# Differential attention: the causal mask of the maxima pass, by VectorE in PSUM or by matmuls with the identity

## The reference, cut to what matters

```python
q = (x @ Wq).reshape(Bz, Tl, H, 2, D)      # H = 8, D = 32: 16 score maps a sequence of Tl = 512
k = (x @ Wk).reshape(Bz, Tl, H, 2, D)
v = (x @ Wv).reshape(Bz, Tl, H, 2 * D)
causal = jnp.tril(jnp.ones((Tl, Tl), dtype=bool))
def attend(qc, kc):
    s = jnp.einsum('bthd,bshd->bhts', qc, kc) * scale
    s = jnp.where(causal, s, -jnp.inf)
    a = jax.nn.softmax(s, axis=-1)
    return jnp.einsum('bhts,bshe->bthe', a, v)
o1, o2 = attend(q[..., 0, :], k[..., 0, :]), attend(q[..., 1, :], k[..., 1, :])
o = o1 - lam * o2                            # then a norm over 64 channels, g, and @ Wo
```

## Time and profile before

| What | Value |
|---|---|
| median of three runs | 2410.3 us (2406.4 to 2411.33) |
| the profiled execution: its time | 2407.47 us |
| its span, first to last instruction | 2405.7 us |
| PE busy | 2087.0 us (87%) |
| DVE busy | 1228.1 us (51%) |
| ACT busy | 749.2 us (31%) |
| mean granted TensorE clock | 0.903 |
| the four maxima stages begin at (first L2297) | 1148.3 us in the first chunk, 1910.67 us in the last |

### The profile page before, as it was taken

The page is one execution under the profiler, slowest core; times in us unless marked ns, Lnnn a source line. Parts: engine busy times, 40 slices in busy tenths (PEclk is TensorE's granted clock), DMA queues, the critical chain, the costliest instruction groups (busy, mean ns, idle before and its releaser), DMA issues. The chain is left out here.

```text
span 2405.7 us, 29600 instructions
## 1 busy us (share of the span) xinstructions
PE 2087.0 (87%) x12078; PEld 996.0 (41%) x12078; DVE 1228.1 (51%) x2281; ACT 749.2 (31%) x1163; POOL 221.2 (9%) x164
## 2 busy tenths in 40 slices
PE   4777486878877479999999999989998999999998
PEld 3444333333435234444444444434443444444443
DVE  5444445657554445555557445653566356623332
ACT  4444123333242122223234322442235123511211
POOL 3341021211110000000100010001000000000000
PEclk7777577988785589999999999999999999999999
DMA  6211402021112212222111111111111111222322
GB/s 247 88 53 18 164 10 48 22 37 28 31 49 58 93 55 94 97 97 75 41 43 62 36 62 54 53 45 53 53 54 53 53 39 34 78 88 98 114 92 74
DMA packets 90978, 158.75 MB, mean 66 GB/s; under 512 B 44182, under 2 KB 55772, under 8 KB 86108
## 3 DMA queue, kind: packets, MB, share of 16 engines
q1 hardware_dynamic: 90844, 156.86, 20.3%
HBM read 128.52 MB, written 18.87 MB: 61 GB/s over the span
## 5 line engine op out<-in xcount | busy, mean ns | idle before, releaser
L1130 PE MATMUL ps<-arena 128*128 128x512 f16 (+1 forms) x4512 | 1019.1, 381 | 19.8 <-DVE arena L1893 12.9
L1130 PEld LDWEIGHTS ps<-arena 128*128 128x128 f16 x4512 | 437.2, 99 | 541.4 <-issue 48.5
L1838 PE MATMUL ps<-arena 128*128 128x512 f16 x1536 | 348.9, 383 | 29.5 <-DVE arena L1884 16.3
L1838 PEld LDWEIGHTS ps<-arena 128*128 128x128 f16 x1536 | 147.4, 98 | 207.3 <-issue 29.2
L1860 ACT ACTIVATE arena<-ps,arena 128x512 f32<-128x512 f32 x128 | 87.6, 684 | 362.3 <-PE ps L1130 362.0
L1893 DVE SCALAR_TENSOR_TENSOR arena<-arena,ps 128x512 f32<-128x512 f32 x128 | 87.9, 686 | 210.1 <-ACT arena L1860 209.5
L2447 ACT ACTIVATE arena<-ps 128x1024 f32<-128x1024 f32 (+3 forms) x128 | 90.1, 704 | 253.7 <-PE ps L2356 253.7
L2552 DVE CAST arena<-arena 128x1024 f16<-128x1024 f32 (+3 forms) x128 | 66.6, 520 | 149.7 <-ACT arena L2447 147.7
L2518 DVE TENSOR_REDUCE arena<-ps 128x2 f32<-128x256 f32 (+3 forms) x128 | 99.6, 819 | 65.1 <-PE ps L2300 65.1
L1902 DVE SCALAR_TENSOR_TENSOR arena<-ps,arena 128x512 f32<-128x512 f32 x128 | 95.8, 748 | 39.3 <-PE ps L1130 39.1
L1921 DVE SCALAR_TENSOR_TENSOR arena<-ps,arena 128x512 f32<-128x512 f32 x64 | 44.0, 687 | 139.6 <-PE ps L1838 139.4
(11 more groups left out here) (267 smaller groups left out, 2466.5 us busy)
## 6 DMA issues: line engine op xcount, KB each, us to landing
arena<-wug_dram SPq DMA_DIRECT2D x128, 512.0 KB, 3.3
arena<-wd_hi_dram SPq DMA_DIRECT2D x16, 1024.0 KB, 5.0
arena<-wd_lo_dram SPq DMA_DIRECT2D x16, 1024.0 KB, 7.3
arena<-arena SPq DMA_DIRECT2D x144, 64.0 KB, 2.1
wug_dram<-arena SPq DMA_DIRECT2D x4, 2048.0 KB, 16.5
arena<-_attn_hidden_states_dram SPq DMA_DIRECT2D x4, 1024.0 KB, 11.8
arena<-in_L_ffn_W_up_dram SPq DMA_DIRECT2D x8, 512.0 KB, 4.4
arena<-in_L_ffn_W_down_dram SPq DMA_DIRECT2D x4, 1024.0 KB, 8.0
```

The lines of the kernel that those rows point to most:

```text
L1130: ins = pe.matmul(out, left[a](c), right[b](c), start=(at == 0), stop=(at == 3 * n - 1))
L1838: ins = pe.matmul(k.ps[:, bank, :], act[x][:, slot, cols], wd[y][:, f, :], start=(f == 0 and m == 0), stop=(f == 7 and m == 2))
```

## The change

On TensorE the four identity matmuls of each unit are gone, and c_score is raised by the score matmuls. On VectorE each of the two halves of a unit first adds the mask to the last 128 columns of its two banks, in place in PSUM, and then reduces the banks. A link stands between the two, since the reduction reads what the addition writes.

```diff
         for r in range(4):
             rows = slice(32 * r, 32 * r + 32)
-            pe.matmul(k.ps[:, max_bank(n, r), 0:w], k.qk_hi[rows, b, u * P:w], k.qk_hi[rows, 4 + b, 0:w],
-                      start=True, stop=False)
-        for r in range(4):
-            ins = pe.matmul(k.ps[:, max_bank(n, r), w - P:w], k.identb, k.causal_ts, start=False, stop=True)
+            ins = pe.matmul(k.ps[:, max_bank(n, r), 0:w], k.qk_hi[rows, b, u * P:w], k.qk_hi[rows, 4 + b, 0:w],
+                            start=True, stop=True)
             if r % 2:
                 ins.then_inc(s["c_score"], 1)
@@
             bank = max_bank(n, 2 * j)
             e.wait_ge(s["c_score"], 2 * UNITS * i + 2 * n + j + 1)
+            edge = k.ps[:, bank:bank + 2, u * P:(u + 1) * P]
+            V.link(e.tensor_tensor(edge, edge, bcast(k.causal_ts.unsqueeze(1), [P, 2, P]), ALU.add))
             e.tensor_reduce(k.mx[:, u, 4 * b + 2 * j:4 * b + 2 * j + 2], k.ps[:, bank:bank + 2, 0:(u + 1) * P], AXX,
                             ALU.max).then_inc(s["c_max"], 1)
```

## The result

The changed kernel takes 2434.23 us in the median of four runs (2431.96 to 2436.11), the kernel before 2410.17 (2406.4 to 2411.33, four runs). The ratio is 1.0105, with a 95% interval of 1.0089 to 1.0121: slower by 1.05%, and the medians lie 24.1 us apart. The forecast was 2441, the range 2423 to 2449.

A forecast was written before the change was run, and what follows sets the result against it. TensorE bounds the kernel, but waits for VectorE's reductions in loops of the maxima stages. Waits of 13.8 us plus clock loss of 17 make 31 us, added to 2410.3 for 2441 us; range 2423 to 2449.

The forecast's parts named there:

- The bound: Maxima stages: TensorE waits for VectorE's reductions in a loop, so VectorE's time counts there despite its 51% mean load.
- TensorE's saving: Identity matmuls removed from the maxima units: 0.23 us for each of 64 units, 14.7 us of TensorE time.
- The addition's price: VectorE's mask addition in PSUM: 0.418 us plus 0.035 for the link, x = 0.45 us each, two a unit.
- the case of a dear write: Rival: VectorE's write to PSUM makes x 0.55 to 0.7 us, giving 2446 to 2458 us; chance 0.10.
- The steps: Times between maxima units: unit 1 to 2 +0.74, 2 to 4 +0.62, 4 to 5 −0.23; a four-unit period +1.13 us.
- the sum: Maxima stage, clock aside: 3 x 1.13 − 0.23 + 0.74 − 0.46 = 3.44 us a chunk, 13.8 us for four.
- The end of the stage: Unit 15's maxima before the transposes: VectorE 0.67 later, TensorE 0.46 earlier, still covered with 0.5 of 1.6 us left.
- The clock: Maxima stages: 12 stops growing to 2.2 us lower TensorE's clock behind 10 of them, costing 17 us, bounds 0 and 20.

The follow-up runs named there:

- the filled kernel: Changed kernel with eight more 512-column matmuls, result thrown away, ahead of the projections following units 3, 7 and 11 of each chunk: 2419.22 us, ratio to before 1.0054.
- the experiment without the mask: Changed kernel without VectorE's additions, so the maxima pass has no mask at all: 2401.35 us, ratio 0.9978 to the kernel before.

## Why the prediction was right, point by point

**The bound.** That TensorE's loop through VectorE decides, and not the 51% of VectorE, was right. The order of widths alone, with no instruction more or less, moved the changed kernel from 24 us over the kernel before to 6 us under it, and the kernel before by 14.

**TensorE's saving**, 0.23 us a unit: shown by the steps bound by TensorE, 4.39 to 4.17 us.

**The addition's price**, x = 0.45: the instruction took 427 ns instead of the 418 taken, and the reduction started 0.46 to 0.47 behind it. The write to PSUM, for which no row stood, costs next to nothing more, so the case of a dear write is out. Ahead of L1893 VectorE still idles 0.52 us of the 1.45, so the additions of the 384-wide unit don't delay it, as forecast.

**The steps.** +0.74, +0.62 and −0.23 a period were forecast; the rows give +0.71, +0.63 and −0.22, a period of 15.15 us. Filling the stops left these alone, which separates the waits from the clock: a stage of the filled kernel is 3.40 us longer than one before, where the sum had 3.44. The end of the stage is covered, as forecast: from unit 15's scores at 1988.37 to the transposes at 1993.90 there is no wait in the last chunk.

**The clock.** Ten falls of twelve had been taken, as an estimate, and the stretches show ten, at 1.7 us each. That it was ten is luck: stops of 2.06 us, with the additions on top of the identity matmuls, gave six of twelve. The ground on which ten was chosen did not hold either. It was that the stop of 3.18 us, with unbroken wide matmuls on both sides, had held, and that those among short breaks and narrow matmuls fell. But the stop of 3.18 us cost clock in four of the seven experiments (its 24 matmuls took 6.81 to 7.04 us instead of 5.36), and that of 1.77 us, with the same work around it each time, held or fell. That the falls in the stages come from the stops is shown by the filling; what decides whether a given stop costs clock stays open. The rule of the Trainium skill ("TensorE: Matmul & The Clock Gate", "Why this matters for your kernels"), by which only longer gaps take the clock down, does not hold here: stops of 2.1 and 2.2 us did, and elsewhere 1.77.

**Where the forecast was off.** It said +31, the median +24. The stages themselves came out as forecast: the first from 1145.63 (unit 0) to 1212.74 (the transposes) is 67.1 us, before it was 1207.0 − 1148.3 = 58.7, so +8.4; the last, 1928.42 to 1993.90, is 65.5, +6.8. The second is like the first and the third like the last, which makes 30.4. The step that failed is that the rest of the kernel was taken as unchanged. In the profiled execution the rest took 6 us less than before: unit 0 begins 2.7 us earlier, and the stops of 1.77 us of the earlier trace rows are still there but the clock held behind them (TensorE of the changed kernel):

```profile
1319.25 2.77 PE L1130 MATMUL ps<-arena 128*128 128x512 f16 x12 [1.76 <-DVE arena L1893]
...
1581.76 2.77 PE L1130 MATMUL ps<-arena 128*128 128x512 f16 x12 [1.77 <-DVE arena L1893]
```

That is 2 x 1.7 = 3.4 us. The 2.7 us ahead of the first stage lie where both kernels issue the same instructions; the cause is not settled. It is no more than executions differ by anyway: over the nine kernels traced, one execution each, all with the same instructions up to there, unit 0 begins between 1142.99 and 1151.31 us. In the same way the experiment without the mask and the one with additions in the even units won more in their stages (12.5 and 7.2 us) than in their medians (5.6 and 3.8).

## What to carry to other kernels

Work moved off the bound engine is a gain only if it isn't in a loop that this engine waits for: lay both engines' time lines side by side, look for each place where the bound engine starts 0.14 us behind the other's end, and price an addition there in full. Elsewhere it costs nothing as long as the other engine's idle time holds it: additions in the even units alone, each with 18 matmuls behind it, lengthened no wait for the reductions. Where such a loop has unequal steps, first try to place the long items where the other engine has most to do; that needed no new instruction and took 14 us off the kernel before. And a wait of 2 us costs more than its length where the clock falls behind it, here 1.7 us each time. Price such falls as a range: how many there will be could not be told beforehand, and parts of the kernel that nobody touched moved by several microseconds too.

## What the runs showed of the hardware that was not expected

- Useless work can make a kernel faster: 96 matmuls more took the changed kernel from 24 to 12 us over the kernel before, since the clock held at 2.4 GHz.
- Stops of the same length, at the same place of the program, sometimes cost the clock and sometimes not. Over the nine kernels traced, one execution each: the 48 stops of 1.13 to 1.28 us in the maxima stages never did, those of 2.06 us six times of 12 and those of 2.21 us ten times of 12. The stop of 1.76 us between the stages held in all three chunks of the changed kernel and fell in all three without the mask; the one of 3.18 us fell in four kernels of nine, and those of 3.77 us fell always.
- So a part of the kernel that a change leaves alone can cost some microseconds more or less, at 1.7 us a fall, which is as large as many effects that one wants to measure. One trace of each kernel can't tell whether the change shifts these falls or whether they differ from execution to execution; executions of the kernel before alone lay between 2398.92 and 2412.37 us. Compare the changed stage itself, and not only the medians.
- A float32 tensor_tensor of 256 elements that reads and writes PSUM took 427 ns, against 418 for one that writes SBUF.
